# One-hot matrices on ACT, an unstaged scatter and spread padding in a four-layer GNN kernel

## What is computed

```python
# layer 0
m = jnp.concatenate([h[edge_src], w], axis=1)
tmp = jax.nn.relu(m @ W1.T + b1)
h_N = jax.ops.segment_sum(tmp, edge_dst, num_segments=h.shape[0])
...
# layer 1
messages = xt[edge_type, col]
out = jax.ops.segment_sum(messages, row, num_segments=num_nodes)
...
# layer 2
e = jax.nn.leaky_relu(a_src[src] + a_dst[dst], NEG_SLOPE)
...
msg = xh[src] * alpha[:, :, None]
out = jax.ops.segment_sum(msg, dst, num_segments=N).reshape(N, H * D) + bias
...
# layer 3
h = jax.ops.segment_sum(w[:, None] * x[col], row, num_segments=N)
```

## Time and profile before

| | us |
|---|---|
| median of 3 runs | 6081.16 |
| lowest and highest | 6079.21, 6087.14 |
| the profiled execution | 6079.68 |
| its span in the profile | 6077.9 |
| mean granted TensorE clock | 0.687 of full speed |

### The profile page before, as it was taken

How to read it: one execution, slowest core, us unless ns; L and a number is a source line. 1 busy time by engine, 2 the same in 40 slices (tenths; PEclk the granted TensorE clock), 3 DMA queues, 4 the chain that set the end, 5 groups by cost and what they waited for, 6 DMA issues and landing times. The chain is left out here.

```text
span 6077.9 us, 105529 instructions
## 1 busy us (share of the span) xinstructions
PE 4177.9 (69%) x13042; PEld 2356.4 (39%) x13047; DVE 3308.1 (54%) x9348; ACT 1044.9 (17%) x3316; POOL 4144.7 (68%) x4253
## 2 busy tenths in 40 slices
PE   4505666666646960889898747666666549989887
PEld 1302333333432430333333336555555423333334
DVE  7316666666432321444444457777777864444445
ACT  0203333333430100000000042222222210000002
POOL 2666777777676777777777617777777257777773
PEclk8756777777778985665555578787888755555557
DMA  1203444434303430444444524444444334444444
GB/s 51 64 24 85 103 103 103 103 103 102 46 3 100 153 108 17 106 105 105 105 105 106 95 67 104 100 101 101 100 101 102 41 108 105 105 105 105 105 105 90
DMA packets 762437, 552.69 MB, mean 91 GB/s; under 512 B 569127, under 2 KB 654846, under 8 KB 762105
## 3 DMA queue, kind: packets, MB, share of 16 engines
q0 software_dynamic: 184832, 443.09, 27.7%
q1 hardware_dynamic: 576888, 106.39, 8.8%
q10 hardware_dynamic: 640, 2.40, 0.1%
HBM read 467.71 MB, written 83.62 MB: 91 GB/s over the span
## 5 line engine op out<-in xcount | busy, mean ns | idle before, releaser
L897 PE MATMUL psS_plain_src<-got_plain_src,hot_plain_src 128*128 128x257 f32 x3328 | 1869.5, 674 | 547.2 <-DVE hot_plain_src L737 272.6
L897 PEld LDWEIGHTS psS_plain_src<-got_plain_src,hot_plain_src 128*128 128x128 f32 x3328 | 790.0, 294 | 1626.7 <-DVE sums L718 799.1
L718 DVE TENSOR_TENSOR sums<-sums,psS_plain_src 128x257 f32 x1664 | 704.2, 423 | 1138.0 <-PE psS_plain_src L897 1119.6
L668 POOL DMA_INDIRECT got_attend_dst<-dram_gtab,recs_attend_dst x832 | 850.2, 1022 | 299.5 <-issue 157.0
L668 POOL DMA_INDIRECT got_edge_mlp_dst<-dram_ptab,recs_edge_mlp_dst x832 | 840.9, 1011 | 284.7 <-ACT msg_edge_mlp_dst L852 131.8
L668 POOL DMA_INDIRECT got_plain_src<-dram_htab,recs_plain_src x832 | 817.4, 982 | 254.3 <-issue 155.9
L668 POOL DMA_INDIRECT got_plain_src<-dram_xtab,recs_plain_src x832 | 814.9, 979 | 254.3 <-issue 153.4
L502 POOL DMA_INDIRECT dram_rec_src<-stage_rec_src x784 | 768.9, 981 | 296.4 <-issue 216.2
L897 PE MATMUL psS_edge_mlp_dst<-msg_edge_mlp_dst,hot_edge_mlp_dst 128*128 128x256 f32 x1664 | 645.1, 525 | 296.0 <-DVE sage_sums L718 243.4
L897 PE MATMUL psS_attend_dst<-msg_attend_dst,hot_attend_dst 128*128 128x264 f32 x1664 | 619.5, 460 | 63.8 <-DVE sums L718 58.4
L897 PEld LDWEIGHTS psS_edge_mlp_dst<-msg_edge_mlp_dst,hot_edge_mlp_dst 128*128 128x128 f32 x1664 | 372.2, 250 | 497.8 <-DVE sage_sums L718 220.4
(11 more groups left out here) (287 smaller groups left out, 3691.7 us busy)
## 6 DMA issues: line engine op xcount, KB each, us to landing
dram_xtab<-out_tab SPq DMA_DIRECT2D x48, 1024.0 KB
recs_plain_src<-dram_rec_src SPq DMA_DIRECT2D x1664, 4.0 KB
recs_edge_mlp_dst<-dram_rec_dst SPq DMA_DIRECT2D x832, 4.0 KB
got_edge_mlp_dst<-dram_ptab,recs_edge_mlp_dst POOLq DMA_INDIRECT x832
got_plain_src<-dram_xtab,recs_plain_src POOLq DMA_INDIRECT x832
recs_attend_dst<-dram_rec_dst SPq DMA_DIRECT2D x832, 4.0 KB
got_attend_dst<-dram_gtab,recs_attend_dst POOLq DMA_INDIRECT x832
got_plain_src<-dram_htab,recs_plain_src POOLq DMA_INDIRECT x832
```

What stands on the lines that cost most here:

```text
L668: nc.gpsimd.indirect_dma_start(got[:, u, 0:w], None, table, bass.IndirectOffsetOnAxis(rec_i[:, u, index_word:index_word + 1], 0)).then_inc ...
L718: nc.vector.tensor_tensor(here, here, psS[t[1] % banks][:, 0:cols], ALU.add).then_inc(added, 1)
L897: nc.tensor.matmul(psS[t[1] % banks][:, 0:cols], hot[:, t[1], :], rows(t), start=True, stop=True).then_inc(sums, 1)
```

## The change

Three things are changed.

1. In `edge_mlp`, `plain` and `attend` (all four passes that run) the one-hot matrix is made by ACT. DVE still makes `rel`, with the operands turned round (base minus node), and now waits for ACT's use of `rel` two groups back. ACT adds 0..127 to it and takes the absolute value (`Abs`, four instructions of 128 by 128 with `rel` as bias, into `gap`), and one step later relu(1 - gap) over the four (`Relu`, 128 by 512, bias `ones`): 1 where gap is 0, else 0. SP now frees record slots by `rels`. In `attend` ACT's `hotT` copy moves from tile t to tile t-2 of the same step.
2. `Scatter.run` has no copy: the DMAs read the records where they are. Its loop is written out in full, 784 DMA instructions with fixed addresses.
3. Padding records get table rows by their column (an `iota` on POOL ahead of the other fills) in place of row 0.

```diff
-            nc.vector.memset(src_i[:, :], 0 if by_dst else int(sh.NOWHERE))
+            nc.gpsimd.iota((src_i if by_dst else dst_i)[:, :], pattern=[[1, COLS]], base=0, channel_multiplier=0)
...
-                nc.gpsimd.tensor_copy(edges.stage_rec[:, h, :, :], edges.rec[:, bass.ds(column, half), :]).then_inc(self.staged, 1)
-                pool.wait_ge(self.staged, 2 * i + h + 1)
-                self.gate.step()
                 for k in range(half):
+                    column = U * (self.first + i) + half * h + k
                     nc.gpsimd.indirect_dma_start(
...
-                    sp.wait_ge(hots, fours(old))
+                    sp.wait_ge(rels, fours(old))
...
+                if hot_on_act:
+
+                    wait_count(dve, gaps, fours_before(t, 2))
+                    here, base = base, here
+                nc.vector.tensor_tensor(rel[:, u // 4 % 2, :], here, base, ALU.subtract).then_inc(rels, 1)
...
+            def one_hot(i, u):
+
+                if (t := ring.at(i, u)) is not None and u % 4 == 0:
+                    act.wait_ge(rels, fours(t))
+                    wait_count(act, hots, fours_before(t, 2))
+                    for k in range(4):
+                        last = nc.scalar.activation(gap[:, u // 4 % 2, k, :], c.iota[:, :], ACT.Abs, bias=rel[:, u // 4 % 2, k:k + 1])
+                    last.then_inc(gaps, 1)
+                if (t := ring.at(i, u, 1)) is not None and t[1] % 4 == 0:
+                    act.wait_ge(gaps, fours(t))
+                    wait_count(act, sums, ring.count((t[0], t[1] + 3), U))
+                    nc.scalar.activation(hot[:, t[1]:t[1] + 4, :], gap[:, t[1] // 4 % 2, :, :], ACT.Relu,
+                                         bias=c.ones[:, 0:1], scale=-1.0).then_inc(hots, 1)
...
                 def step(i, u):
+                    if hot_on_act:
+                        one_hot(i, u)
...
-                    if (t := ring.at(i, u)) is not None:
+                    if (t := ring.at(i, u, 2)) is not None:
                         act.wait_ge(turned, ring.count(t))
                         wait_count(act, nodes, ring.count(t, 4))
-                        nc.scalar.copy(hotT[:, u % 4, :], psF[u % 2][:, 0:P]).then_inc(hotTs, 1)
+                        nc.scalar.copy(hotT[:, t[1] % 4, :], psF[t[1] % 2][:, 0:P]).then_inc(hotTs, 1)
```

More of the change, by code:

```diff
@@ L212, in __init__ @@
         self.begins = sb("begins", [P, sh.COLS], BF16)
-        self.stage_rec = sb("stage_rec", [P, 2, U // 2, REC])
         self.to = c.rec_dst if kind == "dst" else c.rec_src
@@ L316, in link @@
                 dve.wait_ge(chain, chained[0])
-            nc.vector.memset(src_i[:, :], 0 if by_dst else int(sh.NOWHERE))
             if by_dst:
                 nc.vector.memset(next_i[:, :], int(sh.NOWHERE))
-            nc.vector.memset(dst_i[:, :], int(sh.NOWHERE) if by_dst else 0).then_inc(zeroed, 1)
+            nc.vector.memset((dst_i if by_dst else src_i)[:, :], int(sh.NOWHERE)).then_inc(zeroed, 1)
             nc.vector.memset(allone[:, :], 1.0)
@@ L483, in __init__ @@
         if end > first:
-            self.staged = nc.alloc_semaphore(f"staged_{edges.kind}_{first}")
             self.left = [nc.alloc_semaphore(f"left{h}_{edges.kind}_{first}") for h in range(2)]
@@ L490, in run @@
         nc, edges, half = self.nc, self.edges, U // 2
-        def a_round(i):
+        rounds = self.end - self.first
+        for i in range(rounds):
             for h in range(2):
-                column = U * (self.first + i) + half * h
-                if not (isinstance(i, int) and i == 0):
+                if i:
                     pool.wait_ge(self.left[h], 16 * half * i)
                     self.gate.step()
-                nc.gpsimd.tensor_copy(edges.stage_rec[:, h, :, :], edges.rec[:, bass.ds(column, half), :]).then_inc(self.staged, 1)
-                pool.wait_ge(self.staged, 2 * i + h + 1)
-                self.gate.step()
                 for k in range(half):
+                    column = U * (self.first + i) + half * h + k
                     nc.gpsimd.indirect_dma_start(
-                        edges.to, bass.IndirectOffsetOnAxis(edges.stage_rec[:, h, k, PLACE:PLACE + 1].bitcast(I32), 0),
-                        edges.stage_rec[:, h, k, :], None).then_inc(self.left[h], 16)
-        rounds = self.end - self.first
-        a_round(0)
-        if rounds > 1:
-            with pool.Fori(1, rounds) as i:
-                a_round(i)
+                        edges.to, bass.IndirectOffsetOnAxis(edges.rec[:, column, PLACE:PLACE + 1].bitcast(I32), 0),
+                        edges.rec[:, column, :], None).then_inc(self.left[h], 16)
         for h in range(2):
@@ L547, in edge_pass @@
         rels = sem("rels")
+        hot_on_act = mode in ("plain", "edge_mlp", "attend")
+        gap = sb("gap", [P, 2, 4, P], F32) if hot_on_act else None
+        gaps = sem("gaps")
         rec_in = [sem(f"rec_in{s}") for s in range(U)]
@@ L726, in begin @@
                     dve.wait_ge(rec_in[s_], 16 * (t[0] + 1))
-                nc.vector.tensor_tensor(rel[:, u // 4 % 2, :], rec[:, u:u + 4, 1],
-                                        base_f[:, bass.ds(ring.count(t) - 1, 4)], ALU.subtract).then_inc(rels, 1)
+                here, base = rec[:, u:u + 4, 1], base_f[:, bass.ds(ring.count(t) - 1, 4)]
+                if hot_on_act:
+                    wait_count(dve, gaps, fours_before(t, 2))
+                    here, base = base, here
+                nc.vector.tensor_tensor(rel[:, u // 4 % 2, :], here, base, ALU.subtract).then_inc(rels, 1)
             def one_hot(i, u):
                 t = ring.at(i, u)
-                if t is None or u % 4:
+                if hot_on_act or t is None or u % 4:
                     return
@@ L832, in _ @@
         def _(act):
+            def one_hot(i, u):
[10 more added lines that the diff above has]
+                                         bias=c.ones[:, 0:1], scale=-1.0).then_inc(hots, 1)
+            if mode == "plain" and hot_on_act:
+                ring.run(act, one_hot, lag=1)
             if mode == "edge_mlp":
```

## The result

The changed kernel takes 6238.64 us (median of 4 runs, 6235.1 to 6246.39) against 6082.22 us of the kernel before (4 runs, 6079.21 to 6087.14): 1.0258 of its time, 95% interval 1.024 to 1.0276. The forecast was 6195 us, slower, in a range of 6050 to 6370. The profiled execution has a span of 6233.2 us, 155 more than the 6077.9 before.

What follows compares the result with a forecast made beforehand. POOL's DMA issues were taken to bound the plain passes and edge_mlp to within 5%. From 6079.7 us, -74 + 1 - 53 - 18 + 215 + 45 gave 6196, taken as 6195 us; range 6050 to 6370.

Steps and rivals of the forecast that it cites:

- The chain rel, four Abs, spread, transpose, psE, pre: In edge_mlp: a closed chain, once per group of four tiles, that DVE can't run ahead of; 2.64 us.
- B: Rival: chain as forecast, but ACT runs each short Abs in 0.11 us; 5938 us in all, 7%.
- C: Rival: Abs instructions don't overlap, 0.40 us each, so groups in edge_mlp and attend lengthen; 6363 us in all, 10%.
- Edge_mlp, +215: Edge_mlp pass: a round of 16 tiles grows from 21.06 to 25.4 us, over 52 rounds, less about 10 of tail.
- the four `pre` and four `add`: DVE's part of each edge_mlp group: eight instructions, each 0.335 us behind the other, 2.68 us.
- Attend, +45: Attend pass: chain rel, Abs, Relu, transpose, scores, L770 makes a round 22.9 us against 22.1, over 52 rounds.
- Scatter, iota, plain passes: 98 copies gone from the scatter stages, -74 us; iota at most +1; plain gathers without DVE collisions, -25 and -28.
- the floor: POOL's gather issue: 0.949 us plus 0.30 idle behind each, given as 1.254 us a tile.
- Padding: End of each plain pass: different table rows avoid the backlog of tiles; -9 us each, -18 in all.
- A: Rival: ACT is early enough and the chains in edge_mlp and attend are hidden; 5802 us in all, 6%.
- D: Rival: the plain passes don't get faster, something else holding the port or PE's pace being next; 6248 us, 6%.
- Signs: Six marks expected in the changed profile: scatter spacing, plain gathers, last add, edge_mlp idle and gathers, attend's L770, Abs price.

Runs made afterwards that it cites:

- either cut: Changed kernel with, in edge_mlp, ACT's spread ahead of the four Abs (5864.8 us), or PE's four psE ahead of the new group's transpose (5948.89 us).
- z_half_sum: Changed kernel, but in edge_mlp PE sums 128 of the 256 msg columns, leaving out half of that pass's sums: 6152.53 us, 1.0127 of the kernel before.
- v_ahead_2: Changed kernel with spread ahead of the Abs in edge_mlp; in attend rel and Abs one group earlier, Relu two steps earlier: 5773.84 us, 0.9485.
- y_attend_act: Kernel before with attend's part alone: one-hot tiles built by ACT, hotT two steps behind; 6079.4 us against 6076.49, 1.0007.
- x_edge_dve: Changed kernel with the one-hot tiles of edge_mlp alone built by DVE again: 5935.25 us, 0.9755 of the kernel before.
- the first two kernels: Kernel before with only the scatter and padding parts (5952.16 us, 0.9797), and with only the plain passes' one-hot tiles on ACT (6006.28 us, 0.9884).
- y_plain_act: Kernel before with one part alone, the plain passes' one-hot tiles built by ACT: 6006.28 us, 0.9884.

## Why the prediction came out as it did

**Direction and mechanism were right.** The chain rel, four Abs, spread, transpose, psE, pre is there as written (2.47 us; predicted 2.64), opens with either cut, and grows with what is put on it. The prices behind it held: an `Abs` takes 390 ns (predicted 401), and they follow each other by 0.28 to 0.30 (0.29), which ends rivals B and C. The Trainium skill's page "ScalarE: Activation LUTs", section "What ACT_TABLE_LOAD costs", gives about 280 ns + 0.833 a column for an ACTIVATE with a pointer bias and an overlap of about 93; that is 387 and 0.29, and the traces agree. The same page's rule "Use VectorE, not ScalarE" (section "Rules for kernel authors") doesn't hold here: with the order mended, edge_mlp takes 54 us less with its one-hot tiles on ACT than with DVE's. The rule speaks of an instruction's price, and here the engine with idle time is the cheaper one.

**Edge_mlp, +215 against +308: the mis-sized term is the four `pre` and four `add`.** The prediction took them at 0.335 us each, 2.68 a group, from rows in which PE had the sums ready. It looked at PE's clock for the chain's 0.25 us alone and held PE's pace for the sums hidden. So the sums, 0.85 us apart, come just too late for adds 0.67 apart, and the eight take 3.2 us or more. From `rel` to `rel` the looped round is 8.84 + 5.66 + 6.74 + 6.08 = 27.3 us in the mean, where 25.4 was forecast; with half the columns it is 25.6. Over the pass, the gathers' spacing gives (1.680 - 1.316) x 831 = 302 us, where 226 was forecast, and z_half_sum gave 86 of these back. The tail, forecast 10 shorter, is 6 longer: 24.1 us against 18.1. Together that is 92 of the 93 us.

**Attend, +45 against +3.** The chain is 3.46 us from `rel` to L766 (predicted 3.64), as this timeline of the changed kernel has it; it answers the earlier trace rows:

```profile
4210.61 0.17 DVE L724 TENSOR_TENSOR rel_attend_dst<-base_dst,recs_attend_dst 128x4 f32<-128x4 f32 x1
...
4210.81 1.28 ACT L835 ACTIVATE gap_attend_dst<-iota,rel_attend_dst 128x128 f32<-128x128 f32 x4 [0.83 <-DVE rel_attend_dst L724]
...
4212.24 0.72 ACT L840 ACTIVATE hot_attend_dst<-gap_attend_dst,ones 128x512 f32<-128x512 f32 x1
...
4213.09 0.33 PE L958 MATMUL psF_attend_dst<-ident,hot_attend_dst 128*128 128x128 f32 x1 [1.38 <-ACT hot_attend_dst L840]
...
4214.07 0.17 DVE L766 TENSOR_TENSOR z_attend_dst<-psN_attend_dst,got_attend_dst 128x16 f32<-128x16 f32 x1 [0.21 <-PE psN_attend_dst L951]
```

A round is 7.17 + 5.56 + 4.54 + 4.97 = 22.25 us where 7.4 + 14.7 + 0.8 was forecast. Each term was 3% too long, and that is 34 of the 45 us; 3 more are a slip in the sum, since (22.9 - 22.1) x 52 is 42. The term is a small difference between a known round and one built up from a dozen prices, and its sign was never sure. That this chain does set the round, as the prediction said, v_ahead_2 shows.

The measured +3 is one pair of traces, and it is less firm than it looks. The pass took 1153.5 to 1171.8 us in the three traces with DVE's tiles and 1174.8 to 1200.1 in the seven with ACT's and the same order, 21 us more in the mean, while the totals of y_attend_act say +3. What makes attend differ between kernels without an edit in it is open. It is also why the parts run alone don't add up: -124 - 70 + 3 and, from x_edge_dve, +303 make +112, not +156. Pass by pass they do: -75 for the scatter, -21.5 and -57.7 for the plain passes, -10.9 for edge_mlp's tail, +318.9 for its one-hot tiles (1455.9 - 1137.0) and +3 for attend make +157. The rest is attend where its program is unchanged: 18 and 11.5 us less in the first two kernels, and 25 more in x_edge_dve than in the changed kernel.

**Scatter, iota, plain passes** came within 5 us: the plain passes gained 3.8 and 4.6 more than forecast, of which the floor gives 3 each, 1.254 us in the prediction (its own 0.949 + 0.30 make 1.249) and 1.250 in the trace. **Padding**: the two plain tails gave 9.8 and 11.7 (9 each). "In the other two nothing is counted" was wrong for the kernel before, where edge_mlp's tail lost 11, but right in the changed kernel, where the chain's own backlog hid it.

**Rivals.** A (5802) is what the change would have been with both chains open, and v_ahead_2 (5774) is that kernel. It lost by the order of ACT's and DVE's work, as argued. D was excluded by y_plain_act.

**Signs.** Scatters, plain gathers, tails and the price of an `Abs` came as listed. In edge_mlp DVE's idle time before one `pre` in four is 2.3 us (2.4), but the gathers are 1.68 us apart, not 1.55 to 1.6; in attend L766 waits for PE, but a tile takes 1.387 us, not 1.43.

## What to carry to other kernels

An engine that works in order turns every wait into a wait of all that stands behind it. When work moves to an idle engine, ask first which of its old instructions others wait for, put these ahead of the new ones, and start the new ones a group early: here the same instructions were worth +2.6% or -5.1% by their order alone. Where a closed chain slows the loop, price also what hung on the pace of the engines beside it, since their clock may go down with the loop.
